# Softmax attention with 8-wide heads: the value products of a pair of steps issued ahead of the transpositions

## The reference, cut to what matters

```
q, k, v = split(x @ w_attn + b_attn)        # heads: (B, 16, T, 8)
q, k = rope(q), rope(k)
att = einsum('bhqd,bhkd->bhqk', q, k) / sqrt(8)
att = softmax(where(causal, att, -inf))
y = einsum('bhqk,bhkd->bhqd', att, v)
return y @ w_proj + b_proj
```

## Time and profile before

| | us |
|---|---|
| time, median of 3 runs (2548.55 to 2553.3) | 2550.59 |
| the profiled execution's own time | 2554.86 |
| its span, first to last instruction | 2552.9 |
| TensorE busy | 2318.2 (91%) |
| first to last matmul of the changed stage | 251.8 to 599.2 |

### The profile page before, as it was taken

One profiled execution on the slowest core, in us unless ns is written; L12 is line 12 of the kernel. 1 busy time (PEld: TensorE's weight loads), 2 busy tenths in 40 slices (PEclk: granted clock), 3 DMA queues, 4 the chain that ended last, 5 costly groups with the idle time before them and its releaser, 6 DMA issues. The chain is left out here.

```text
span 2552.9 us, 65073 instructions
## 1 busy us (share of the span) xinstructions
PE 2318.2 (91%) x21430; PEld 1706.7 (67%) x21430; DVE 1856.7 (73%) x4076; ACT 1807.9 (71%) x5998; POOL 1479.3 (58%) x1404
## 2 busy tenths in 40 slices
PE   5497999998198999999999999898999999999998
PEld 4495666665197688874688874574688864788863
DVE  2394788884187699984799975585799974899974
ACT  3254688885053899984799984434899983999982
POOL 2672577772465487771578770240677770777750
PEclk7698799999599999999999999999999999999999
DMA  6111000000112100000000000000000000000000
GB/s 276 45 48 48 1 1 0 0 1 1 36 44 66 63 7 8 6 4 4 6 9 6 8 3 0 2 0 3 10 7 8 6 3 4 8 8 6 8 1 33
DMA packets 30611, 51.07 MB, mean 20 GB/s; under 512 B 6064, under 2 KB 24496, under 8 KB 29712
## 3 DMA queue, kind: packets, MB, share of 16 engines
q1 hardware_dynamic: 25936, 40.09, 4.8%
q0 software_dynamic: 4544, 9.35, 1.1%
HBM read 24.45 MB, written 16.59 MB: 16 GB/s over the span
## 5 line engine op out<-in xcount | busy, mean ns | idle before, releaser
L271 POOL TENSOR_TENSOR l_tS<-l_t,tabs 128x512 f32<-128x512 f32 x256 | 325.6, 1272 | 247.3 <-DVE l_t L370 231.0
L296 ACT ACTIVATE l_pr<-psum,l_nm 128x128 f32<-128x128 f32 x1024 | 357.6, 360 | 8.4 <-DVE l_nm L374 8.4
L268 POOL TENSOR_TENSOR l_pr<-l_pr,l_rl 128x512 f32<-128x512 f32 x256 | 266.2, 1040 | 163.6 <-DVE l_rl L358 163.6
L275 POOL TENSOR_TENSOR l_t<-l_t,l_tS 128x512 f32<-128x512 f32 x256 | 325.4, 1271 | 23.9 <-POOL l_tS L271 7.6
L182 PE MATMUL psum<-l_hT,big 128*128 128x256 f32 x1024 | 266.0, 382 | 12.3 <-DVE l_t L370 12.0
L883 POOL TENSOR_TENSOR ss_pr<-ss_pr,ss_rl 128x256 f32<-128x256 f32 (+1 forms) x256 | 221.1, 884 | 93.5 <-DVE ss_rl L986 91.4
L354 DVE CAST psum<-cb 128x512 f32<-128x512 bf16 x256 | 177.9, 695 | 88.1 <-ACT l_pr L296 88.1
L929 ACT ACTIVATE ss_pr<-psum,ss_nm 128x128 f32<-128x128 f32 (+1 forms) x512 | 210.0, 443 | 9.0 <-DVE ss_nm L979 9.0
L205 PE MATMUL psum<-l_sq,cf 128*128 128x384 f32 x512 | 209.9, 492 | 1.8 <-DVE l_qk L340 1.2
L296 ACT ACTIVATION_READ_ACCUMULATOR l_pr<-psum,l_nm 128x1 f32 x1024 | 205.8, 201 | 0.0
L182 PEld LDWEIGHTS psum<-l_hT,big 128*128 128x128 f32 x1024 | 175.8, 191 | 30.1 <-issue 16.6
(11 more groups left out here) (179 smaller groups left out, 5656.6 us busy)
## 6 DMA issues: line engine op xcount, KB each, us to landing
big<-early SPq DMA_DIRECT2D x1, 6688.0 KB, 37.6
ex_xb<-sorted SPq DMA_DIRECT2D x78, 64.5 KB
z<-token_y SPq DMA_DIRECT2D x16, 256.0 KB, 6.0
l_hT<-z SPq DMA_DIRECT2D x64, 64.0 KB, 1.9
l_hT<-z SPq DMA_DIRECT2D x64, 63.8 KB, 2.0
sorted<-z SPq DMA_DIRECT2D x2, 1999.5 KB, 18.7
big<-late SPq DMA_DIRECT2D x1, 3114.0 KB, 11.2
cf<-const SPq DMA_DIRECT2D x1, 2089.5 KB, 12.4
```

Source lines behind the costliest of these rows:

```text
L268: pool.tensor_tensor(x, x, rl[:, (j - 3) % 2, :, :].rearrange("p h t -> p (h t)").unsqueeze(2).to_broadcast([P, 4, P]), ALU.mult).then_inc ...
L271: pool.tensor_tensor(tS[:, :], t2[:, :], tab[:, 1, :], ALU.mult).then_inc(ts_ready, 1)
L275: pool.tensor_tensor(t3[:, j % 2, :], t1[:, j % 2, :], tS[:, :], ALU.add).then_inc(summed, 1)
L296: ins = act.activation(pr[:, (j - 3) % 2, h, t * P:(t + 1) * P], s_ps[h][:, t * P:(t + 1) * P], ACT.Exp, bias=nm[:, (j - 3) % 2, h, t:t + ...
```

## The change

In the loop body of TensorE the block that issues the value products (L840 to L855 of the kernel before) now stands directly behind the scores, ahead of projection, values and transpositions. Its waits, operands and signals are unchanged. As the value products are issued in odd steps alone, and projection and values at e = 0 and e = 4 alone, the issued order differs in odd steps only: scores, value products, transpositions, where it was scores, transpositions, value products.

```diff
                         ins.then_inc(s_ready, 1)
 
-                    if runs(b + 1, B):
-                        if e == 0:
-                            project(b + 1)
-                        if e == 4:
-                            values(b + 1)
-
-                    u = s - 3
-                    if runs(u, U):
-                        kk, ee = place(k, e, 3)
-                        pe.wait_ge(normed, u + 1)
-                        if at_least(u, 1):
-                            pe.wait_ge(pt_low, u)
-                            pe.wait_ge(pt_high, u)
-                        for h in range(2):
-                            for c in range(3):
-                                ins = nc.tensor.transpose(pt_ps[h][:, c * P:(c + 1) * P], pr[:, ee % SLOTS, h, c * P:(c + 1) * P], g.ident32)
-                        ins.then_inc(pt_ready, 1)
-
                     u = s - 5
                     if e % 2 and runs(u, U):
                         kk, ee = place(k, e, 5)
...
                         ins.then_inc(pv_ready, 1)
+
+                    if runs(b + 1, B):
+                        if e == 0:
+                            project(b + 1)
+                        if e == 4:
+                            values(b + 1)
+
+                    u = s - 3
+                    if runs(u, U):
+                        kk, ee = place(k, e, 3)
+                        pe.wait_ge(normed, u + 1)
+                        if at_least(u, 1):
+                            pe.wait_ge(pt_low, u)
+                            pe.wait_ge(pt_high, u)
+                        for h in range(2):
+                            for c in range(3):
+                                ins = nc.tensor.transpose(pt_ps[h][:, c * P:(c + 1) * P], pr[:, ee % SLOTS, h, c * P:(c + 1) * P], g.ident32)
+                        ins.then_inc(pt_ready, 1)
```

More of the change, by code:

```diff
@@ L820, in body @@
                         ins.then_inc(s_ready, 1)
+                    u = s - 5
+                    if e % 2 and runs(u, U):
+                        kk, ee = place(k, e, 5)
+                        jj = ee // 2
+                        pe.wait_ge(pt_low, u + 2)
+                        pe.wait_ge(pt_high, u + 2)
+                        if ee == 0:
+                            pe.wait_ge(v_ready, b + 1)
+                            if at_least(b, 1):
+                                pe.wait_ge(out_ready, b)
+                        for q0, col, n, kt in ((0, 0, T, 0), (P, T, P, 1)):
+                            for q in range(4):
+                                cs = slice(32 * q, 32 * q + 32)
+                                ins = mm(ol[cs, q0:q0 + n], vm[:, kk, kt, jj * P + 32 * q:jj * P + 32 * q + 32], pt[:, (ee + q // 2) % SLOTS, q % 2, col:col + n],
+                                         start=(jj == 0 and kt == 0), stop=(jj == 3 and kt == 1), skip_group_check=True)
+                        ins.then_inc(pv_ready, 1)
                     if runs(b + 1, B):
@@ L838, in body @@
                         ins.then_inc(pt_ready, 1)
[L840 to L855, removed]
             project(0)
```

## The result

| | before | after |
|---|---|---|
| time, median of 6 runs each, us | 2550.94 (2546.91 to 2554.21) | 2574.06 (2571.26 to 2576.21) |
| profiled execution: time, span | 2554.86, 2552.9 | 2575.30, 2573.2 |
| one batch in the steady part of the stage | 20.65 | 21.93 |

The ratio is 1.0093 (95% interval 1.008 to 1.0106): 0.9% slower, 23 us. The prediction was slower by 8 us, 2552 to 2565; the sign is right, the size is not, and the time lies above the range.

What follows compares the result with a forecast made beforehand. TensorE was taken to bound the stage, with ACT having 14% to spare. The terms 6.3 + 1.5 + 0.2 + 0.2 = 8.2 us took the median from 2550.6 to 2558.8 us, range 2552 to 2565.

Steps and rivals of the forecast that it cites:

- the hole at e = 7: TensorE's 0.56 us wait before the transpositions, once a batch; value products wait for the same copies, so cannot fill it.
- The gain from fewer array shapes: Odd steps on TensorE: three changes between array shapes instead of four, 0.1 us less for each odd step.
- ACT's copy ahead of the exponentials: Odd steps: transpositions end later, so ACT's copy and exponentials start later; the mask of e = 3 comes 0.38 us late.
- the pairs of the last batch: Last batch, without projection, values or query copies: each pair of steps takes 5.04 us against 4.66, 1.5 us in all.
- One sign: In the changed profile, ACT's wait for the transpositions was to rise from 29.7 us by 20 or more.
- The two query copies: VectorE, behind the copy of e = 5: two masked copies of the queries, taken at 1.76 us.
- the maxima and reciprocal behind them: VectorE, maxima and reciprocal of e = 6 behind the query copies, taken at 1.01 us.
- the list: One batch laid out step by step from the scores of e = 1, engines as in the trace; 0.45 us more a batch.
- ready just in time: GpSimd's sum, awaited by the query copies, was to move as much as VectorE's reciprocal (ready at 404.11 before).
- the 0.45 of the prediction: The loss in us for each batch with a projection, 14 x 0.45 = 6.3 us.
- the draining behind it: Steps behind the last batch: 0.2 us, last exponentials 0.7 later, mostly hidden behind GpSimd's division.
- Every odd step stalls: Rival: projection and values don't give ACT its time back; 1.5 us a batch, 23 us, 2573 us; chance 0.08.

Runs made afterwards that it cites:

- q_before: The kernel before with VectorE's masked query copies spread over e = 5, 6, 7 and the next e = 0: 2540.59 us, ratio 0.9969.
- short_div_before: The kernel before with GpSimd's division cut from 128 and 256 columns a head to 8 and 8: 20.05 us a batch, ratio 0.9972.

## Why the prediction was wrong

*That the hole at e = 7 would not be filled: right.* The counts waited for are the same, and the value products of e = 7 stand idle 0.80 us where the transpositions stood 0.56. The spread of the query copies shows that the holder was VectorE's queue, and short divisions close the hole too, since they make the query copies short.

*The gain from fewer array shapes: right.* Transpositions and mask now start 0.72 us apart in odd steps without a wait, and at e = 1 it takes 1.51 us from the first block behind the scores to the mask (393.81 to 395.32) where it took 1.59 (392.53 to 394.12). With the mask 0.02 us shorter that is the 0.1 us of the prediction. At e = 7 alone it is 0.07.

*ACT's copy ahead of the exponentials: right in mechanism and size.* The mask of e = 3 waits for L929, the one of e = 5 does not, the pairs of the last batch take 5.03 us (5.04). One sign failed: ACT's wait for the transpositions rose from 29.7 to 38.0 us over the stage, not by 20 or more. ACT waits for VectorE's maxima instead, 24.7 us where it was 9.0.

*The step that failed: VectorE's pieces were taken over at the durations they had before.* The two query copies, "1.76", and the maxima and reciprocal behind them, "1.01", came out as written (1.77 and 1.01 us in the changed kernel). What failed stands ahead of them. The 0.85 and 0.88 us of L957 and L964 are no terms of the list at all; at e = 1 and e = 3 they were moved as blocks of fixed length. In truth these pieces started 0.3 us before the end of a narrow piece of GpSimd's division and took 0.17 to 0.20 us more than alone (0.68). Behind a copy that comes later they meet a wide piece with 0.9 to 1.0 us left. The sines, which the list would have had end at 401.90 (its 399.24, then 0.03, 0.47 and 0.88, moved by 1.28 as above), ended at 402.90. That makes the maxima and the reciprocal of e = 4 late, and with them the division and GpSimd's rotated sum, on which the query copies wait. The prediction had that sum "ready just in time", with 0.47 us from the copy of e = 5 to the query copies:

```profile
405.57 1.27 POOL L872 TENSOR_TENSOR ss_qk<-z 128x512 f32<-128x512 f32 x1
```

```profile
406.12 0.56 DVE L993 COPY z<-psum 128x384 f32<-128x384 f32 x1 [0.32 <-PE psum L854]
406.96 1.84 DVE L970 TENSOR_SCALAR ss_qz<-ss_qk,cf 128x256 f32<-128x256 f32 x2 [0.29 <-POOL ss_qk L872]
```

It took 0.84 us. The copy of e = 5 was laid at 405.60 and came at 406.12, the query copies were laid at 406.07 and came at 406.96, 0.89 us late, and the value products of e = 7 were 0.87 us late. That was the missing 0.83 us a batch: 21.93 measured, 21.10 forecast. In b = 1 and b = 14, where the sines did not wait, the query copies start right behind the copy, and the loss was 0.40 and 0.41 us, near the 0.45 of the prediction. With the wide piece moved out of the way the changed order takes 21.08. That nearness is partly luck, since the query copies shift against GpSimd too.

The Trainium skill states the rule, "SBUF — State Buffer", section "Who interferes with whom": a VectorE instruction with two SBUF inputs contends with a GpSimd instruction that reads SBUF. That whoever issues first holds the shared ports for the whole instruction, while the other blocks fully, that section of the Trainium skill says of VectorE's two-port modes. The traces show the same for the two-input pieces here: wherever they were stretched they ended 0.55 us after the end of a GpSimd piece that ran when they started, and GpSimd's wide piece waited in its turn where VectorE was first. The query copies, which read one tensor, wait as well and end 0.15 us after the piece. The prediction did not weigh this rule, though it bore on every piece that the change moves.

*The total.* In the profiled executions the stage, from its first projection to the end of its last value product, went from 347.3 to 364.0 us, 16.7 more. Twelve steady batches give 1.28 us each, 15.4, and the ones before and behind them 0.4 each. The prediction had taken all fourteen as equal, while b = 1 and b = 14 took 20.56 us before and not 20.64. The last batch gives 1.6, and the draining behind it 1.4, where the prediction had 0.2. The start of the stage at half clock was 2.5 us shorter. 1.8 of it lie in the first batch, where the clock rose at 274 us and not at 281; 0.7 lie between the first two projections, which stand 8.1 or 8.8 us apart in kernels with the old order as well (8.81 in before, 8.82 in q_before, 8.09 in short_div_before). In q_before and short_div_before the clock rose between 275 and 276 and at 274, so the profile of before had a long case, and the stage's own loss is nearer 19 us. What comes ahead of the stage took 1.7 us less in the profile of after, and what comes behind it 5.3 us more; over all profiles of these kernels that part takes 1949 to 1959 us, so such differences are common. Whether about 4 of the 23 us are such scatter or belong to the change stays open.

*The rivals.* "Every odd step stalls" gave 2573, next to the measured 2574, but for another reason: the pair with the projection does not stall for ACT. It had been given 0.08. Its nearness is no credit to it.

## What to carry to other kernels

When an instruction moves in time, its duration is only kept if no instruction that it can block, or be blocked by, moves relative to it (here VectorE's two-input pieces and GpSimd's division): before taking a duration from a row, look at what the partner engine ran at its start, and lay out both engines' pieces, not one. An in-order engine that waits twice for the same count gains next to nothing by swapping the two waiters (0.12 us a batch here); it delays the signals of the one put behind. A hole is filled by finding which queue made its releaser late, here one masked copy too many ahead of the maxima.

## What the runs showed of the hardware

The same VectorE instruction (128 x 512, two SBUF inputs) took 0.68 us alone, 0.85 to 0.88 when it started 0.3 us before the end of a narrow GpSimd piece, and 1.27 to 1.57 when it started 0.7 to 1.0 us before the end of a wide one. With 0.11 us of a narrow piece left it took 0.68, and the wide piece behind took 1.51 us in place of 1.04. A query copy (128 x 256, one tensor) took 0.34 us alone and up to 1.12 beside a wide piece. GpSimd's small copy L865 took 0.39 us before and 0.86 in the changed kernel, where it met the rotation piece. TensorE's weight loads of the mask follow those of the transpositions without idle time, both on the full array, while the matmuls of the transpositions still run (395.91 against 396.18 in the kernel before).
